# Another order of the steps around the expert units of a hybrid attention, RWKV and mixture-of-experts kernel

## What is computed

```
x = x + attention(layernorm(x))     # one head, causal softmax, scores over 512 tokens
x = x + moe(layernorm(x))           # 32 experts, the best 4 of each token, swiglu, hidden 64,
                                    # capacity 2048 pairs an expert, and one shared expert, hidden 128
x = x + rwkv(layernorm(x))          # layer norm, shift by a token, k, v, r, the wkv recurrence,
                                    # output product; then channel mixing: square(relu(xk Wkey)) Wval,
                                    # gated by a sigmoid
x = x + moe(layernorm(x))           # the same experts again
```

## Time and profile before

| | |
|---|---|
| runs of the kernel before | 897.68, 905.74, 906.85 us |
| the profiled execution | 905.0 us, its span 903.2 us |
| PE busy | 822.2 us (91%) |
| PE weight loads busy | 617.6 us (68%) |
| DVE busy | 684.3 us (76%) |
| POOL busy | 609.4 us (67%) |
| ACT busy | 522.6 us (58%) |
| mean granted TensorE clock | 0.965 |

### The profile page before, as it was taken

One profiled execution on the slowest core, in us unless ns is written; L12 is line 12 of the kernel. 1 busy time (PEld: TensorE's weight loads), 2 busy tenths in 40 slices (PEclk: granted clock), 3 DMA queues, 4 the chain that ended last, 5 costly groups with the idle time before them and its releaser, 6 DMA issues. The chain is left out here.

```text
span 903.2 us, 12742 instructions
## 1 busy us (share of the span) xinstructions
PE 822.2 (91%) x3846; PEld 617.6 (68%) x3846; DVE 684.3 (76%) x1567; ACT 522.6 (58%) x974; POOL 609.4 (67%) x465
## 2 busy tenths in 40 slices
PE   3589999889989989898999999998999979999997
PEld 2367787656666666576777667776777857777775
DVE  4548777698798897897569885797758988875754
ACT  2247575554755647456666674756746466585653
POOL 5418686674756757756777758766676768776865
PEclk8589999999999999999999999999999999999999
DMA  9033343324214332145152614443253423525353
GB/s 312 0 96 95 75 106 70 84 48 97 74 35 124 75 88 68 46 97 117 46 109 50 162 48 97 106 94 72 59 125 90 97 52 78 118 59 136 87 129 76
DMA packets 48228, 81.26 MB, mean 90 GB/s; under 512 B 3360, under 2 KB 12704, under 8 KB 47776
## 3 DMA queue, kind: packets, MB, share of 16 engines
q1 hardware_dynamic: 47872, 80.24, 36.9%
q10 hardware_dynamic: 288, 0.20, 0.1%
HBM read 75.72 MB, written 4.72 MB: 89 GB/s over the span
## 5 line engine op out<-in xcount | busy, mean ns | idle before, releaser
L471 POOL TENSOR_TENSOR m_h<-m_v,m_wb 128x512 f32<-128x512 f32 x256 | 350.0, 1378 | 173.9 <-DVE m_v L1077 79.7
L569 ACT ACTIVATE m_th<-pa 128x512 f32<-128x512 f32 x232 | 137.5, 594 | 120.0 <-PE pa L782 113.9
L1077 DVE TENSOR_TENSOR m_v<-m_th,pb 128x512 f32<-128x512 f32 x216 | 145.0, 678 | 38.3 <-ACT m_th L569 18.0
L780 PE MATMUL pa<-m_xh,w1h 128*128 128x512 f32 x272 | 144.0, 529 | 0.1
L714 ACT ACTIVATE m_hh<-m_h 128x512 fp32r<-128x512 f32 x180 | 113.0, 628 | 42.5 <-POOL m_h L471 41.3
L342 POOL TENSOR_TENSOR m_hl<-m_h,m_hh 128x512 fp32r<-128x512 f32 x76 | 103.4, 1361 | 44.4 <-ACT m_hh L714 44.4
L342 DVE TENSOR_TENSOR m_hl<-m_h,m_hh 128x512 fp32r<-128x512 f32 x104 | 85.3, 821 | 53.3 <-ACT m_hh L714 52.7
L780 PE MATMUL pb<-m_xh,w3h 128*128 128x512 f32 x272 | 111.6, 410 | 8.1 <-DVE m_v L1077 6.5
L782 PE MATMUL pa<-m_xh,w1l 128*128 128x512 f32 x272 | 108.5, 399 | 0.0
L782 PE MATMUL pb<-m_xh,w3l 128*128 128x512 f32 x272 | 108.2, 398 | 0.0
L781 PE MATMUL pb<-m_xl,w3h 128*128 128x512 f32 x272 | 108.0, 397 | 0.0
(11 more groups left out here) (211 smaller groups left out, 1601.2 us busy)
## 6 DMA issues: line engine op xcount, KB each, us to landing
m_wb<-w_scratch SPq DMA_DIRECT2D x126, 512.0 KB, 6.7
x_sb<-in_x SPq DMA_DIRECT2D x8, 256.0 KB, 7.2
m_wb<-in_w SPq DMA_DIRECT2D x2, 1024.0 KB, 7.0
x_out<-x_sb SPq DMA_DIRECT2D x8, 256.0 KB, 6.8
u_scratch<-t_u SPq DMA_DIRECT2D x6, 256.0 KB, 2.7
t_u<-u_scratch SPq DMA_DIRECT2D x6, 256.0 KB, 2.9
f_kk<-in_w SPq DMA_DIRECT2D x1, 1024.0 KB, 10.0
w_scratch<-r_wT SPq DMA_DIRECT2D x16, 64.0 KB, 1.6
```

What stands on the lines that cost most here:

```text
L471: pool.tensor_tensor(hidden(g, p), gated(g, p), m_wb[:, p % (GRING * GP), :], ALU.mult).then_inc(sig["m_h"], 1)
L569: ins = act.activation(m_th[:, p % 2, :], pa[p % 2][:, :], ACT.Silu)
L780: pe.matmul(ps[:, :], high[:, p, :], xh, start=True, stop=False)
L1077: dve.tensor_tensor(gated(g, p), m_th[:, r, :], pb[r][:, :], ALU.mult).then_inc(sig["m_v"], 1)
```

## The change

Almost every tuple of slots is replaced. No instruction is added or taken away by that; the steps of attention, routing, time mixing and channel mixing stand behind other units, by mode, on all four engines. In attention, PE's third and fourth score blocks are issued with the turns and values one slot apart from before. Two tables change too: unit 13 of mode 3 (g = 6, 8, 10) is split instead of native, and POOL takes the low part of unit 10 in mode 3, of units 3 and 7 in mode 5, and of 0 and 1 instead of 2 in mode 6.

The slots of some steps, before and after, by mode:

| step | mode 1 | mode 3 | mode 2 |
|---|---|---|---|
| `out_turn` on PE | 3, 6 | 7, 7 | 4, 4 |
| attention: turn, products, scores on PE | 2, 4, 6; 5, 7, 9 | | |
| attention: first maximum, exponential, turn | 6, 8, 9; 9, 10, 10 | | |
| attention: last maximum, exponential, turn | 13, 13, 14; 13, 13, 13 | | |
| routing: norm (ACT), turn (PE), copies (ACT), logits (PE) | 6, 7, 7, 8; 7, 7, 7, 8 | 5, 8, 7, 8; 3, 8, 7, 9 | 7, 9, 9, 9; 6, 7, 6, 8 |
| routing: m_xl (POOL) | 6; 6 | 6; 8 | 6; 5 |
| routing: exponential, top four, counts | 8, 10, 12; 8, 10, 12 | 9, 10, 12; 11, 11, 13 | 9, 9, 12; 9, 11, 13 |
| time: mixes (DVE), K, V, R (PE) | 6, 9, 9, 10; 7, 9, 9, 11 | 7, 8, 9, 10; 7, 8, 9, 12 | 6, 8, 9, 10; 6, 7, 9, 10 |
| time: scan (DVE), exponents (ACT) | 9, 11; 9, 11 | 9, 9; 10, 11 | 8, 9; 7, 10 |
| time: first, other inversions (DVE) | 13, 15, 16; 14, 15, 16 | | 16, 16, 17; 15, 16, 17 |
| channel: norm (ACT), turn (PE), keys (PE) | | 7, 7, 9, 9, 11, 11; 7, 8, 10, 10, 11, 12 | 6, 7, 10, 11, 14, 15; 8, 9, 12, 13, 15, 15 |

In mode 6 the routing of the last pair moves from logits at 10, counts at 12 and turned weights at 14 to 6, 8 and 12. In mode 5 the output product moves from 1 to 5, and channel mixing's turn and keys from 6, 12, 12, 13 and 14 to 11, 14, 14, 14 and 14.

The diff, with the lines of the tuples alone:

```diff
@@ tables @@
-NATIVE = ((9,), (1, 3, 5, 7, 9, 11, 13, 15), (1, 3, 5, 7, 9, 11, 13, 15), (1, 3, 5, 7, 9, 13, 15), (1, 3, 5, 7, 9, 11, 13, 15), (1,), (9, 13))
-LOW_ON_POOL = ((4, 6, 7, 8, 11, 12, 14, 15), (4, 6, 8, 12, 14), (6, 10, 14), (6, 11, 14), (0, 6, 8, 12, 14), (0, 6, 9, 12, 15), (2, 4, 8, 14))
+NATIVE = ((9,), (1, 3, 5, 7, 9, 11, 13, 15), (1, 3, 5, 7, 9, 11, 13, 15), (1, 3, 5, 7, 9, 15), (1, 3, 5, 7, 9, 11, 13, 15), (1,), (9, 13))
+LOW_ON_POOL = ((4, 6, 7, 8, 11, 12, 14, 15), (4, 6, 8, 12, 14), (6, 10, 14), (6, 10, 11, 14), (0, 6, 8, 12, 14), (0, 3, 6, 7, 9, 12, 15), (0, 1, 4, 8, 14))
@@ gpsimd: pro_step @@
-if slot == (4, 3, 0, 1, 0, 3, 2)[mode]:
+if slot == (2, 4, 0, 0, 0, 2, 0)[mode]:
-if slot == (8, 6, 6, 6, 14, 10, 10)[mode]:
+if slot == (7, 6, 5, 8, 14, 14, 11)[mode]:
@@ gpsimd: time_begin @@
-if slot == (1, 1, 0)[mode]:
+if slot == (0, 1, 1)[mode]:
-if slot == (4, 5, 5)[mode]:
+if slot == (5, 4, 5)[mode]:
-if slot == (9, 7, 7)[mode]:
+if slot == (9, 8, 9)[mode]:
-if slot == (11, 8, 14)[mode]:
+if slot == (10, 9, 13)[mode]:
@@ gpsimd: channel_step @@
-if slot == (14, 16, 13, 11)[mode]:
+if slot == (17, 14, 14, 14)[mode]:
-if slot == (3, 5, 5, 2)[mode]:
+if slot == (3, 5, 5, 5)[mode]:
-if slot == (6, 6, 6, 5)[mode]:
+if slot == (7, 6, 6, 10)[mode]:
...
@@ scalar: att_step @@
-if slot == (4, 1)[mode]:
+if slot == (3, 5)[mode]:
-if slot == (5, 4)[mode]:
+if slot == (4, 9)[mode]:
-if slot == (9, 8)[mode]:
+if slot == (8, 10)[mode]:
-if slot == (11, 9)[mode]:
+if slot == (10, 10)[mode]:
-if slot == (13, 11)[mode]:
+if slot == (11, 13)[mode]:
-if slot == (13, 13)[mode]:
+if slot == (12, 13)[mode]:
-if slot == (15, 13)[mode]:
+if slot == (15, 14)[mode]:
@@ scalar: pro_step @@
-if slot == (6, 6, 7, 5, 4, 7, 5)[mode]:
+if slot == (6, 7, 6, 3, 4, 8, 4)[mode]:
-if slot == (8, 7, 9, 7, 5, 9, 7)[mode]:
+if slot == (7, 7, 6, 7, 5, 12, 5)[mode]:
-if slot == (9, 8, 9, 9, 9, 12, 10)[mode]:
+if slot == (8, 8, 9, 11, 9, 13, 6)[mode]:
-if slot == (14, 13, 14, 15, 15, 17, 14)[mode]:
+if slot == (13, 13, 15, 14, 13, 14, 12)[mode]:
@@ scalar: time_begin @@
-if slot == (3, 4, 3)[mode]:
+if slot == (4, 4, 4)[mode]:
-if slot == (5, 5, 6)[mode]:
+if slot == (6, 5, 6)[mode]:
-if slot == (9, 8, 8)[mode]:
+if slot == (9, 7, 7)[mode]:
-if slot == (9, 9, 9)[mode]:
+if slot == (11, 9, 10)[mode]:
-if slot == (12, 10, 10)[mode]:
+if slot == (12, 11, 12)[mode]:
-if slot == (11, 9, 9)[mode]:
+if slot == (11, 10, 11)[mode]:
@@ scalar: channel_step @@
-if slot == (9, 8, 8, 10)[mode]:
+if slot == (10, 8, 8, 13)[mode]:
-if slot == (6, 7, 6, 5)[mode]:
+if slot == (8, 7, 6, 10)[mode]:
-if slot == (6, 7, 7, 6)[mode]:
+if slot == (9, 7, 6, 11)[mode]:
-if slot == (10, 9, 12, 12)[mode]:
+if slot == (12, 10, 12, 14)[mode]:
-if slot == (13, 9, 12, 12)[mode]:
+if slot == (13, 10, 13, 14)[mode]:
-if slot == (14, 10, 14, 13)[mode]:
+if slot == (15, 10, 13, 14)[mode]:
-if slot == (14, 11, 14, 13)[mode]:
+if slot == (15, 14, 15, 14)[mode]:
-if slot == (15, 14, 15, 14)[mode]:
+if slot == (15, 15, 15, 14)[mode]:
...
@@ tensor: att_step @@
-if slot == (4, 2)[mode]:
+if slot == (3, 5)[mode]:
-if slot == (5, 4)[mode]:
+if slot == (4, 7)[mode]:
-if slot == (6, 6)[mode]:
+if slot == (6, 9)[mode]:
-if slot == (11, 9)[mode]:
+if slot == (10, 10)[mode]:
-if slot == (12, 11)[mode]:
+if slot == (11, 12)[mode]:
+if slot == (11, 13)[mode]:
+scores(n, (3,), (0,))
-scores(n, (3,), (0,))
+values(n, 1, (2,), (0,))
-values(n, 1, (2,), (0,))
-if slot == (14, 14)[mode]:
-if slot == (16, 15)[mode]:
+if slot == (16, 16)[mode]:
@@ tensor: pro_step @@
-if slot == (7, 7, 9, 8, 5, 8, 7)[mode]:
+if slot == (7, 7, 7, 8, 5, 11, 5)[mode]:
-if slot == (9, 8, 9, 8, 7, 11, 10)[mode]:
+if slot == (8, 8, 8, 9, 7, 13, 6)[mode]:
-if slot == (13, 12, 12, 12, 14, 14, 12)[mode]:
+if slot == (12, 12, 13, 13, 12, 14, 8)[mode]:
-if slot == (14, 13, 15, 15, 15, 15, 14)[mode]:
+if slot == (13, 13, 14, 14, 13, 15, 12)[mode]:
@@ tensor: time_begin @@
-if slot == (4, 5, 6)[mode]:
+if slot == (6, 5, 6)[mode]:
-if slot == (9, 8, 8)[mode]:
+if slot == (9, 7, 8)[mode]:
-if slot == (10, 10, 10)[mode]:
+if slot == (11, 10, 12)[mode]:
@@ tensor: time_out @@
-if slot == (1, 2, 3, 1)[mode]:
+if slot == (2, 3, 3, 5)[mode]:
@@ tensor: channel_step @@
-if slot == (7, 7, 7, 6)[mode]:
+if slot == (9, 8, 7, 11)[mode]:
-if slot == (10, 9, 12, 12)[mode]:
+if slot == (12, 10, 12, 14)[mode]:
-if slot == (11, 9, 12, 12)[mode]:
+if slot == (13, 10, 13, 14)[mode]:
-if slot == (14, 11, 14, 13)[mode]:
+if slot == (15, 11, 14, 14)[mode]:
-if slot == (15, 11, 14, 14)[mode]:
+if slot == (15, 12, 15, 14)[mode]:
@@ tensor: iteration @@
-if slot == (4, 3, 4, 7, 4, 6, 4)[it.mode]:
+if slot == (5, 6, 4, 7, 4, 10, 4)[it.mode]:
@@ vector: att_step @@
-if slot == (0, 0)[mode]:
+if slot == (0, 2)[mode]:
-if slot == (2, 0)[mode]:
+if slot == (1, 3)[mode]:
-if slot == (4, 1)[mode]:
+if slot == (2, 3)[mode]:
-if slot == (7, 4)[mode]:
+if slot == (5, 6)[mode]:
-if slot == (12, 12)[mode]:
+if slot == (11, 13)[mode]:
-if slot == (13, 12)[mode]:
+if slot == (11, 13)[mode]:
-if slot == (8, 6)[mode]:
+if slot == (6, 9)[mode]:
-if slot == (11, 9)[mode]:
+if slot == (10, 10)[mode]:
-if slot == (13, 13)[mode]:
+if slot == (11, 13)[mode]:
@@ vector: pro_step @@
-if slot == (4, 3, 0, 1, 0, 3, 0)[mode]:
+if slot == (2, 4, 0, 0, 0, 1, 0)[mode]:
-if slot == (5, 3, 4, 3, 2, 5, 4)[mode]:
+if slot == (5, 6, 1, 2, 1, 7, 1)[mode]:
-if slot == (9, 8, 8, 8, 7, 11, 10)[mode]:
+if slot == (7, 7, 7, 9, 8, 12, 5)[mode]:
-if slot == (9, 10, 9, 9, 10, 12, 10)[mode]:
+if slot == (9, 8, 9, 10, 9, 13, 6)[mode]:
-if slot == (11, 10, 9, 10, 11, 12, 10)[mode]:
+if slot == (10, 10, 11, 11, 10, 13, 6)[mode]:
-if slot == (13, 12, 12, 11, 13, 13, 12)[mode]:
+if slot == (11, 12, 13, 12, 12, 13, 11)[mode]:
@@ vector: time_begin @@
-if slot == (1, 1, 0)[mode]:
+if slot == (0, 1, 1)[mode]:
-if slot == (3, 3, 2)[mode]:
+if slot == (2, 3, 3)[mode]:
-if slot == (6, 6, 7)[mode]:
+if slot == (7, 6, 7)[mode]:
-if slot == (9, 8, 9)[mode]:
+if slot == (9, 7, 10)[mode]:
@@ vector: time_finish @@
-if slot == (13, 13, 12)[mode]:
+if slot == (13, 14, 13)[mode]:
-if slot == (13, 14, 12)[mode]:
+if slot == (13, 14, 13)[mode]:
-if slot == (13, 16, 13)[mode]:
+if slot == (14, 15, 15)[mode]:
-if slot == (16, 17, 15)[mode]:
+if slot == (16, 17, 16)[mode]:
-if slot == (15, 16, 14)[mode]:
+if slot == (15, 16, 15)[mode]:
-if slot == (17, 17, 16)[mode]:
+if slot == (16, 17, 16)[mode]:
...
@@ vector: iteration @@
-if slot == (4, 3, 5, 7, 4, 5, 3)[it.mode]:
+if slot == (5, 6, 6, 7, 4, 10, 3)[it.mode]:
```

More of the change, by code:

```diff
@@ L526, in iteration @@
                             split_low(pool, *before, "m_hl_pool")
-                    if it.att is not None and slot == (0, 0)[it.mode]:
+                    if it.att is not None and slot == (0, 2)[it.mode]:
                         rsqrt(a_rs[:, :], a_ve[:, :], "a_vedone", it.att + 1, "a_rstd")
@@ L728, in iteration @@
                         split_high(*unit_before(g, slot, SPLIT_LAG))
-                    if slot == (2, 2, 3, 3, 3, 3, 3)[it.mode]:
+                    if slot == (3, 3, 2, 3, 3, 3, 3)[it.mode]:
                         out_copy(g)
@@ L1303, in time_out @@
             def time_out(m, slot, mode):
-                if slot == (2, 3, 3, 1)[mode]:
+                if slot == (2, 2, 3, 5)[mode]:
                     dve.wait_ge(sig["t_ops"], m + 1)
@@ L1310, in channel_step @@
             def channel_step(m, slot, mode):
-                if slot == (8, 8, 9, 10)[mode]:
+                if slot == (10, 8, 8, 12)[mode]:
                     dve.wait_ge(sig["f_xh"], m + 1)
                     dve.tensor_tensor(f_xl[:, :], f_xk[:, :], f_xh[:, :].bitcast(F32), ALU.subtract).then_inc(sig["f_xl"], 1)
-                if slot == (3, 1, 3, 2)[mode] and m == 0:
+                if slot == (3, 0, 3, 2)[mode] and m == 0:
                     dve.wait_ge(sig["a_add"], 3 * B)
                     dve.memset(f_h[:, 0:1], 0.0).then_inc(sig["f_zero"], 1)
-                if slot == (3, 5, 5, 2)[mode]:
+                if slot == (3, 5, 5, 5)[mode]:
                     kept(dve, m)
@@ L1321, in channel_step @@
                     dve.tensor_scalar(a_ve[:, 0:T], a_mv[:, :, 1], EPS, None, ALU.add).then_inc(sig["f_ve"], 1)
-                if slot == (5, 5, 5, 3)[mode]:
+                if slot == (6, 5, 5, 8)[mode]:
                     dve.wait_ge(sig["f_rstd"], m + 1)
                     shifts(f_nm[:, :], a_mv, a_rs[:, 0:T], "f_nm")
-                if slot == (7, 7, 8, 7)[mode]:
+                if slot == (8, 7, 7, 11)[mode]:
                     dve.wait_ge(sig["f_d"], m + 1)
@@ L1329, in channel_step @@
                                                  op0=ALU.mult, op1=ALU.add).then_inc(sig["f_xk"], 1)
-                if slot == (17, 17, 17, 17)[mode]:
+                if slot == (17, 16, 16, 17)[mode]:
                     dve.wait_ge(sig["f_tr2"], m + 1)
```

## The result

The changed kernel takes 866.08 us (median of four runs, 864.21 to 867.53) against 904.31 of the kernel before: a ratio of 0.9587, 95% interval 0.953 to 0.9644. The forecast was 886, the range 871 to 905, so the direction was right and the gain, 37 to 38 us, twice the 20 forecast.

A forecast was written before the change was run, and what follows sets the result against it. PE was taken as the bound, DVE second in mode 1, with idle time from handshakes paid again in clock falls. From 905.0 us, -6 - 6.6 - 3 - 1 + 1.5 - 1.5 - 3.4 gave 885.0, rounded to 886; range 871 to 905.

The forecast's parts named there:

- the clock's term: Granted clock: two of mode 1's stretches at half clock taken as gone, -3.4 us, between 0 and -13.6.
- a fall for K: Mode 3, unit 8: K's new PE wait for DVE's mixes, about 2.2 us, was allowed its stretch at half clock.
- (a): Mode 1: turn of the output goes from unit 3 to 6, removing its wait, -0.7 us an iteration.
- (b): Mode 1: ACT's copied turn moves to 13, so t_r comes earlier; 0.7 of each 2.0 us counts' wait kept.
- (d): Mode 1: tighter attention chains cost 0.9 us (first block), 1.3 (last) and 0.8 (scores' input), +3.0 an iteration.
- (c): Mode 1: attention's first steps and maxima leave DVE's crowd at 0 to 6, -2.0 us an iteration.
- (e): Mode 1: DVE, the second bound, gives part of the gain back, +0.3 us an iteration.
- the second rival: Mode 1: attention's short chains cost the uncovered 3.6 us each, with four new clock falls; 920 us, chance 13%.
- the four units between the weighted product and the down product hide it: Outside mode 6: weights moving a slot or two on SP's queue were claimed hidden, with no cost or gain.
- The reason given for mode 6: Mode 6: last weights reach SP's queue 4 us earlier, shortening POOL's DMA wait as the last iteration began; -1.5 us.
- The first: Rival, mode 1: moved DVE mixes and scans collide with POOL, eating the gain, clock falls stay; 894.4 us, chance 27%.
- The third: Rival, whole kernel: waits only change place, nothing measurable; 905 us, within 5, chance 15%.

The follow-up runs named there:

- filler passes: Kernel before with redundant up passes, results unused, ahead of three PE waits: mode 3's turn, mode 1's counts, iteration 12's logits; 892.13 us, ratio 0.9902.
- three half-made orders: Kernel before with parts of mode 1's new order: attention and output turn, 917.87 us; also time mixing's first steps, 911.46; routing's statistics and shift alone, 924.97.

## Why the gain was twice the forecast

Measured are 37.7 us by the table, against the forecast's sum of 20.0. Of the 17.7 us between, the clock's term has 8.5, mode 1 has 7.1 and mode 4 has 4.6; the other lines are off both ways and nearly cancel.

**Clock: the largest miss.** "I take two of the falls of modes 1 as gone: -3.4" should have been seven falls, -11.9. The prediction saw that idle time "is paid for twice", and then credited the second payment only at the counts' wait, though it also removed the waits of mode 3 that stand before four falls. It even reserved a fall for K. In the new order no wait of PE in modes 1 and 3 exceeds 1.1 us, and no fall is left there. The filler passes show the causation, clearly for modes 1 and 2, and the price, 1.7 us each. Part of the size is chance: four falls in mode 3 is the most that any trace of its old order shows, and at 1.7 us each a profile with none would have left 6.8 us less to win. In the repeated comparison the change stands at 0.963 instead of 0.9587. The Trainium skill, "TensorE: Matmul & The Clock Gate", section "What's actually happening", says that the throttled state is the default and activity releases it; the run with filler agrees, as more work on PE gave less time.

**Mode 1: -13.1 for -6.** Iterations 3 and 4 had no fall, so they give the size cleanly: -3.4 and -3.1 where -1.5 was forecast. (a) is right, the wait for `m_y` is gone. (b) kept 0.7 us of the counts' wait; nothing is left. (d) was the closest call and right in kind. PE in iteration 4 after, all its waits over 0.4 us:

```profile
PE pu L869 <- ACT a_p L600: 1.1, 1, 1.1
PE pq L935 <- ACT t_k L644: 0.7, 1, 0.7
PE pu L869 <- issue: 0.7, 1, 0.7
PE pq L938 <- ACT t_v L649: 0.5, 1, 0.5
```

The last block's chain costs 1.1 for 1.3 forecast, the first's 0.7 for 0.9, and the scores' input nothing for 0.8. With these in place the forecast's own sum is -0.7 - 2.0 - 2.0 + 1.8 - 0.8 + 0.3 = -3.4, as measured; but the terms (c) and (e) were not measured apart, so the agreement does not prove each. (The 2.6 us that the prediction takes off for (a) and (b) in its upper bound and in the second rival are 2.0 by its own terms; its forecast does not use them.)

**Mode 4: -5.6 for -1.** The failed step is "the four units between the weighted product and the down product hide it", said of weights that move by a slot. They did not: mode 3's weights are those of the mode 4 iteration that follows, and moving them by one slot is 3.7 of the 5.6 in the traces. Mode 4's own new slots show nothing: with mode 3 alone its iterations are as short. The earlier trace rows had the sign of it, POOL's 39.7 us in fourteen waits for that DMA; the prediction used the row for mode 6 only.

**Mode 3: -8.2 for -6.6, by terms off both ways.** The turn's and the logits' waits went as forecast. K waits 0.57 us in iteration 8 instead of 2.2; so about 1.6 more was won there than forecast and, as only -2.7 an iteration was measured, the keys won about 1.1 less, an inference from the sum. Measured against the old order's iterations without a fall (53.8, 54.0 and 54.4 us in the run with attention alone), the three are 6.7 us shorter, the forecast's size; how the 15.0 divide between waits and clock is uncertain by that 1.5.

**Mode 2: -0.4 for -3.** The old waits did go; POOL's longest before `m_xl` is 3.8 for under 3 forecast. But two new ones came that the prediction did not price, 2.0 us for `m_v` and 1.0 for `x_sb`, and a fall stands behind the first. K, priced at 1.6 us more, waits 1.3 against 1.4 before. PE in iteration 12 after:

```profile
PE pa L780 <- DVE m_v L1089: 2.0, 1, 2.0
PE pq L932 <- DVE t_xr L1247: 1.3, 1, 1.3
PE pv L758 <- DVE x_sb L1098: 1.0, 1, 1.0
```

**Mode 5 and 6** had the right signs, and the forecast priced them at about half. Most of it is one trade: the new mode 5 takes 2.9 us and gives 2.6 back in iteration 14. The reason given for mode 6, the last iteration, is not borne out: it went from 46.4 to 45.2, but takes 45.1 to 45.5 in the ten other traces with mode 6's old order. **Prologue and mode 0**, priced at 0, took 1.7 more, which the executions' own differences cover.

**The rivals.** The first needed DVE to pay for collisions: its busy time in iteration 4 is 50.46 against 50.95, and its whole 7.9 us less. The second needed more than 5 us of waits for `a_p` in an iteration of mode 1; there are 1.8. The prediction set the prologue's waits for `a_p` aside because they "hold table loads". The trace of before shows none at them: ACT loads a table at 1.75 and 61.54 us only, and its exponentials wait 5.3 and 5.5 us for DVE's maxima. The rival's outcome, slower, was near: three half-made orders are 1.4 to 3% slower. Their largest waits, 2.6 to 5.6 us, are for norms and products; for `a_p` PE waits 2.1 and 1.8 us at unit 13 in the two that move attention. The third fell with the time.

**Open** are which other step of mode 3 makes the last 2 us of mode 4, why the same waits bring a fall in one execution and none in another, and what the turn of the output alone is worth in mode 1; it wasn't tried, since attention's first product at 4 has to wait for what that turn's addition brings at 6.

## What to carry to other kernels

Where a fast stretch is interrupted by waits of 2 us, look at the granted clock behind each and put its loss on the price of the wait, here up to 1.7 on top of 2. Look in more than one trace, since one profile may hold more falls than the next. In a hand-made order of several strict queues the places of the steps pay as a set. Routing's later statistics cost 3.0% alone, with the norm behind them left in place, and were part of a step that won 2.1%. So a move that measures badly alone may still belong to the best order, and a chain is to be moved on every engine it runs through. A step that feeds the next iteration through DRAM has its price there: ask who waits for that DMA, and read its waits before calling it hidden.
